# Routed experts: the weights become the stationary operand of gate and up, and the routing weights multiply the down products

## The chip, the cores and the metric

The kernel is one program on one core of a Trainium2 chip, written engine by engine with explicit semaphores: PE (TensorE) multiplies, ACT (ScalarE) and DVE (VectorE) empty PSUM, POOL (GpSimd) gathers, SP (SyncE) issues DMAs. The metric is the time of one execution on the device in microseconds (us), as the median of several runs.

## What is computed

Two transformer layers with gated residual branches. The change touches only the last branch, a mixture of experts (E = 32 experts, D = 256, inner width I = 128, T = 1024 tokens, 4 experts for each token, capacity C = 40 slots for each expert):

```python
G = jnp.einsum('ecd,edi->eci', Xp, W_gate)          # Xp: the C token rows of each expert
U = jnp.einsum('ecd,edi->eci', Xp, W_up)
Y = jnp.einsum('eci,eid->ecd', jax.nn.silu(G) * U, W_down)
Yf = Y.reshape(EC, d) * slots_w[:, None]            # routing weight of the slot
out = jnp.zeros((T, d), x.dtype).at[slots_token].add(Yf)
shared = jax.nn.silu(x @ shared_gate.T) * (x @ shared_up.T) @ shared_down.T
return (out + shared).reshape(b, s, d)
```

## The kernel before

The first layers and the latent attention fill the span up to about 363 us. Then `stage_moe` runs: the last projection, the norm, the router, the shared expert, the lists of slots, and from about 405 us the loop over the routed experts, which the change rewrites.

The loop takes the experts in 16 pairs (`PAIRED`). In a tile of 128 partitions, partitions 0 to 63 belong to the first expert of the pair and 64 to 127 to the second (`DC` = 64, of which 40 are slots). All matmuls of the loop are float32. For pair q:

- POOL gathers the 128 token rows with their routing weights from DRAM into `XR` (L1517).
- `turn_rows` (PE, L1620): two transposes, and ACT copies them to `XG` (`rows_turned`, L1735). `XG` has the input dimension on the partitions and 64 columns for each expert.
- `gate_up` (PE, L1634): for each of the two halves of the input dimension and each expert a matmul with the 64 columns of `XG` stationary and 256 columns of gate and up weights (`EGU`) moving. The result has the 64 slots of an expert on its partitions; the two experts use the two halves of the array's columns.
- `gated` (ACT, L1743): SiLU of the gate part to `SE`.
- `hidden` (DVE, L1891): two instructions of 64 partitions, `HR` = `SE` times routing weight (a column of `XR`) times the up part.
- `turn_hidden` (PE, L1647): one transpose of `HR`, copied by ACT to `HX` (`hidden_turned`, L1750).
- `down` (PE, L1658): two matmuls, the 64 columns of `HX` stationary, 256 columns of `ED` moving.
- `results` (ACT, L1755) writes the high float16 part to `YS`, `second` (DVE, L1900) the rest.
- `pack` (SP, L1456): two or three DMAs for each pair move `YS` to `YP`, in which slots lie without gaps. SP also issues the weights of the last experts (L1424, L1426).

The order of work is written out by hand, and each engine runs its own list in order. On PE:

```python
for q in range(PAIRED):
    if q + 2 < PAIRED:
        turn_rows(q + 2)
    if q + 1 < PAIRED:
        gate_up(q + 1)
    turn_hidden(q)
    if q == 1:
        pe.wait_ge(tok_ok, 1)
    if q >= 1:
        down(q - 1)
down(PAIRED - 1)
```

Before that loop PE runs `turn_rows(0)`, `turn_rows(1)`, `gate_up(0)` and a small transpose of the slot list (L1667), which waits for a DMA. After it comes `scatter` (L1684): 160 float16 matmuls with one-hot matrices add the packed rows to the tokens. The first 128 wait for the packing DMAs of pairs 0 to 12 (`d_pack[0]`), the last 32 for those of pairs 13 to 15. DVE then adds to `X` and SP stores.

Of the kernel before, what the change touches and what calls it, by code (L numbers as in the profile page):

```python
# [14 lines left out]
ALU = mybir.AluOpType  # L15
ACT = mybir.ActivationFunctionType
AX = mybir.AxisListType

P = 128
B, S, D = 4, 256, 256  # L20
T = B * S
NT = T // P
KT = D // P
# [3 lines left out]
DC = 64  # L27
# [13 lines left out]
E, EI = 32, 128  # L41
# [4 lines left out]
EPT = P // CAP  # L46
# [1252 lines left out]
def stage_moe(nc, g, i, out):  # L1299
# [11 lines left out]
    with ExitStack() as ctx:  # L1311
        sb = lambda name, shape, dt=F32: ctx.enter_context(nc.sbuf_tensor(name, shape, dt))
        sem = lambda name: ctx.enter_context(nc.semaphore(name))
        OWN, RING = 7, 9
# [34 lines left out]
        PAIRED = E // 2  # L1349
# [15 lines left out]
        EGU += [in_place(g.XT[:, :, :]), in_place(HS[:, :, :])]  # L1365
        ED += [g.XN[:, EPT * u:EPT * u + EPT, :] for u in range(RING - OWN)]
        SE = [sb(f"SE{u}", [P, EI]) for u in range(2)]
        HR = [sb(f"HR{u}", [P, EI]) for u in range(2)]
        HX = [sb(f"HX{u}", [P, P]) for u in range(2)]
        YS = [sb(f"YS{q}", [P, 2, D], F16) for q in range(PAIRED)]  # L1370
        rows_dram = nc.dram_tensor("token_rows", [T + 1, ROW], F32).ap()
# [6 lines left out]
        def pieces(e):  # L1378

            at, end, some = e * CAP, e * CAP + CAP, []  # L1380
            while at < end:
# [18 lines left out]
                  "sh_ps", "sh_ok"])  # L1400
        FLIGHT = 4
        d_g = [sem(f"d_g{q}") for q in range(FLIGHT)]
        (xt_ps2, xg_ok, gu_ps, se_ok, h_ok, ht_ps, hp_ok, st_ok, y_ps, yh_ok, yl_ok, acc_ps, fin_ok) = map(
            sem, ["xt_ps2", "xg_ok", "gu_ps", "se_ok", "h_ok", "ht_ps", "hp_ok", "st_ok", "y_ps2", "yh_ok", "yl_ok",
                  "acc_ps", "fin_ok"])
        d_pack = [sem("d_pack_early"), sem("d_pack_late")]

# [6 lines left out]
        with nc.Block() as block:  # L1414
# [107 lines left out]
            def _(pe):  # L1522
# [101 lines left out]
                def gate_up(q):  # L1624

                    pe.wait_ge(xg_ok, q + 1)
                    if q >= 2:
                        pe.wait_ge(h_ok, q - 1)
                    for e in (2 * q, 2 * q + 1):
                        pe.wait_ge(d_e[set_of(e // EPT)], landed(e // EPT))  # L1630
                    for k in range(KT):
                        for h in range(2):
                            e = 2 * q + h
                            mm = pe.matmul(g.ps[DC * h:DC * h + DC, GU + q % 2, 0:2 * EI],  # L1634
                                           XG[q % 2][:, k, DC * h:DC * h + DC],
                                           EGU[e // EPT % RING][:, e % EPT, k, :, :].rearrange("p w n -> p (w n)"),
                                           start=(k == 0), stop=(k == KT - 1))
                    mm.then_inc(gu_ps, 1)

                def turn_hidden(q):  # L1640

                    pe.wait_ge(h_ok, q + 1)
                    if q >= 2:
                        pe.wait_ge(hp_ok, q - 1)
                    else:
                        pe.wait_ge(sh_ok, q + 1)
                    pe.transpose(g.ps[:, HTB + q % 2, 0:P], HR[q % 2][:, :], g.ident[:, :]).then_inc(ht_ps, 1)  # L1647

                def down(q):

                    pe.wait_ge(hp_ok, q + 1)
                    if q >= 2:
                        pe.wait_ge(yl_ok, q - 1)
                    else:
                        pe.wait_ge(sh_ok, q + 3)
                    for h in range(2):
                        e = 2 * q + h
                        mm = pe.matmul(g.ps[DC * h:DC * h + DC, Y + q % 2, 0:D], HX[q % 2][:, DC * h:DC * h + DC],  # L1658
                                       ED[e // EPT % RING][:, e % EPT, :], start=True, stop=True)
                    mm.then_inc(y_ps, 1)  # L1660
# [8 lines left out]
                for q in range(PAIRED):  # L1669
                    if q + 2 < PAIRED:  # L1670
                        turn_rows(q + 2)
                    if q + 1 < PAIRED:
                        gate_up(q + 1)
                    turn_hidden(q)
                    if q == 1:
                        pe.wait_ge(tok_ok, 1)
                    if q >= 1:
                        down(q - 1)
                down(PAIRED - 1)

                acc = lambda t: half_bank(ACC, t)
                def scatter(t, n):
# [17 lines left out]
            @block.scalar  # L1700
            def _(act):
                def turned_norm(q):

                    act.wait_ge(xt_ps, q + 1)
                    act.activation(g.XT[:, :, S * q:S * q + S],
                                   g.ps[:, 4 + q % 2, :].rearrange("p (k s) -> p k s", k=KT),
                                   ACT.Copy).then_inc(xt, 1)

                def shared_gate(n):
                    act.wait_ge(gu_sh, 2 * n + 1)  # L1710
                    if n >= 2:
                        act.wait_ge(hs_ok, n - 1)
                    act.activation(SL[n % 2][:, :], g.ps[:, 2 * (n % 2), :], ACT.Silu).then_inc(sl_ok, 1)
                    act.wait_ge(gu_sh, 2 * n + 2)
                    act.activation(UPS[n % 2][:, :], g.ps[:, 2 * (n % 2) + 1, :], ACT.Copy).then_inc(sl_ok, 1)

                for q in range(B - 1):
                    norm_root(act, g, n3, q)
                turned_norm(0)
                turned_norm(1)  # L1720
                norm_root(act, g, n3, B - 1)
                turned_norm(2)
                act.activation(primed[:, :], g.gate[0:1, 0:1], ACT.Sigmoid)
                turned_norm(B - 1)
                act.wait_ge(rl_ps, 1)
                act.activation(SG[:, :, :], g.ps[:, 6, 0:NT * E], ACT.Sigmoid).then_inc(sg_ok, 1)
                for n in range(4):
                    shared_gate(n)

                def rows_turned(q):  # L1730

                    act.wait_ge(xt_ps2, q + 1)
                    if q >= 2:
                        act.wait_ge(gu_ps, q - 1)
                    act.activation(XG[q % 2][:, :, :], g.ps[:, XTB + q % 2, 0:D].rearrange("p (k s) -> p k s", k=KT),  # L1735
                                   ACT.Copy).then_inc(xg_ok, 1)

                def gated(q):

                    act.wait_ge(gu_ps, q + 1)  # L1740
                    if q >= 2:
                        act.wait_ge(h_ok, q - 1)
                    act.activation(SE[q % 2][:, :], g.ps[:, GU + q % 2, 0:EI], ACT.Silu).then_inc(se_ok, 1)  # L1743

                def hidden_turned(q):

                    act.wait_ge(ht_ps, q + 1)
                    if q >= 2:
                        act.wait_ge(y_ps, q - 1)
                    act.activation(HX[q % 2][:, :], g.ps[:, HTB + q % 2, 0:P], ACT.Copy).then_inc(hp_ok, 1)  # L1750

                def results(q):

                    act.wait_ge(y_ps, q + 1)
                    act.activation(YS[q][:, 0, :], g.ps[:, Y + q % 2, 0:D], ACT.Copy).then_inc(yh_ok, 1)  # L1755

                rows_turned(0)
                rows_turned(1)
                gated(0)
                for q in range(PAIRED):  # L1760
                    if q + 2 < PAIRED:
                        rows_turned(q + 2)
                    if q + 1 < PAIRED:
                        gated(q + 1)
                    hidden_turned(q)
                    if q >= 1:
                        results(q - 1)
                results(PAIRED - 1)

            @block.vector  # L1770
            def _(dve):
# [111 lines left out]
                def hidden(q):  # L1883

                    dve.wait_ge(d_g[q % FLIGHT], 16 * (q // FLIGHT + 1))
                    dve.wait_ge(se_ok, q + 1)
                    if q >= 2:
                        dve.wait_ge(ht_ps, q - 1)
                    for h in range(2):
                        rows = slice(DC * h, DC * h + DC)  # L1890
                        ins = dve.scalar_tensor_tensor(out=HR[q % 2][rows, :], in0=SE[q % 2][rows, :],  # L1891
                                                       scalar=XR[q % HOLD][rows, D + 2 * q + h:D + 2 * q + h + 1],
                                                       in1=g.ps[rows, GU + q % 2, EI:2 * EI], op0=ALU.mult,
                                                       op1=ALU.mult)
                    ins.then_inc(h_ok, 1)

                def second(q):

                    dve.wait_ge(yh_ok, q + 1)
                    dve.tensor_tensor(YS[q][:, 1, :], g.ps[:, Y + q % 2, 0:D], YS[q][:, 0, :],  # L1900
                                      ALU.subtract).then_inc(yl_ok, 1)

                hidden(0)
                dve.wait_ge(slot_ps, 2)
# [3 lines left out]
                for q in range(PAIRED):  # L1908
                    if q + 1 < PAIRED:
                        hidden(q + 1)  # L1910
                    if q >= 1:
                        second(q - 1)
                    if 3 <= q < 3 + TILES_S:
                        placed(q - 3)
                second(PAIRED - 1)
                for b in range(B):
                    dve.wait_ge(acc_ps, 2 * b + 2)
                    for t in (2 * b, 2 * b + 1):
# [110 lines left out]
```

## Time and profile before

| | us |
|---|---|
| median of 3 runs (464.79 to 466.34) | 465.26 |
| the profiled execution, time | 466.26 |
| its span, first to last instruction | 464.5 |
| PE busy | 432.4 (93%) |
| DVE busy | 301.3 (65%) |
| ACT busy | 252.4 (54%) |
| POOL busy | 193.9 (42%) |
| routed loop, from the slot transposition to the scatter | 408.57 to 443.34 |

The span leaves out 1.8 us of the execution's own time. Busy time is the time in which an engine has an instruction in flight, so PE at 93% isn't PE at its peak. Weight loads are shown as an engine of their own (PEld). A float32 matmul appears as two instructions, each with its own weight load; a float32 transpose as one.

### The profile page before, as it was taken

The page shows a single profiled execution, that of the slowest core. Times are in us where ns is not written, and L with a number is a line of the kernel's source. Part 1 is how long each engine was busy: PE and PEld are TensorE (multiplying, and loading weights), DVE is VectorE, ACT ScalarE, POOL GpSimd, SP SyncE. Part 2 cuts the span into 40 slices and gives each one's busy share as a digit, 9 for nine tenths or more (in the row PEclk, how much of TensorE's full clock was granted, in tenths as well). Part 3 has the DMA queues.
Part 4 walks back from the last instruction along what each step waited for, and adds up shares of the span by engine and source line. Part 5 has one row for each costly group of instructions (what it writes and reads, how often), then busy time and mean ns, then how long its engine had stood idle before and what let it go on. Part 6 is the DMA issues. An engine that isn't in the chain of part 4 may idle for free. (4 is left out here: it accounts for less than half of the span.)

```text
span 464.5 us, 8843 instructions
## 1 busy us (share of the span) xinstructions
PE 432.4 (93%) x2723; PEld 276.3 (59%) x2723; DVE 301.3 (65%) x880; ACT 252.4 (54%) x629; POOL 193.9 (42%) x195
## 2 busy tenths in 40 slices
PE   5895999989988999999999999999999998889996
PEld 2584787777744555556555555555568773644476
DVE  3979799965247757667676667757744558446613
ACT  3593336364344776767677766776666252145500
POOL 3441314040434556565456655556644425444000
PEclk9996899999999999999999999999999999999999
DMA  7743000000204343443324334212200599789202
GB/s 249 218 97 102 1 1 2 1 1 2 68 0 97 78 107 76 94 122 68 98 71 102 90 76 104 57 44 52 64 23 2 148 308 305 210 203 244 65 30 92
DMA packets 61448, 43.81 MB, mean 94 GB/s; under 512 B 22955, under 2 KB 54502, under 8 KB 61414
## 3 DMA queue, kind: packets, MB, share of 16 engines
q1 hardware_dynamic: 60646, 41.04, 33.2%
q0 software_dynamic: 768, 2.36, 2.6%
q8 instruction: 17, 0.28, 0.3%
q14 instruction: 17, 0.14, 0.1%
HBM read 27.25 MB, written 2.23 MB: 63 GB/s over the span
## 5 line engine op out<-in xcount | busy, mean ns | idle before, releaser
L1206 POOL TENSOR_TENSOR W1T<-W1T,inv 128x512 f32<-128x512 f32 x64 | 66.5, 1039 | 77.4 <-DVE inv L1261 77.4
L1150 ACT ACTIVATE W1T<-ps,low 128x256 f32<-128x256 f32 x128 | 59.5, 470 | 30.8 <-DVE low L1255 30.8
L276 POOL TENSOR_TENSOR rot<-rot 128x512 f32<-128x512 f32 x48 | 61.0, 1270 | 28.7 <-DMA rot<-rot 28.7
L1255 DVE TENSOR_REDUCE low<-ps 128x2 f32<-128x512 f32 x64 | 44.1, 688 | 39.2 <-PE ps L1065 38.6
L1158 ACT ACTIVATE W2T<-ps 128x512 f32<-128x512 f32 x64 | 38.2, 597 | 7.2 <-PE ps L1073 5.2
L1073 PE MATMUL ps<-ident,W1T 128*128 128x128 f32 x256 | 41.1, 283 | 0.9 <-POOL W1T L1206 0.8
L1073 PEld LDWEIGHTS ps<-ident,W1T 128*128 128x128 f32 x256 | 27.8, 141 | 23.7 <-issue 20.3
L256 DVE TENSOR_TENSOR rot<-ps,sinq 128x512 f32<-128x512 f32 x48 | 33.1, 690 | 13.4 <-PE ps L243 11.2
L243 PE MATMUL ps<-XH,CH 128*128 128x512 f16 x96 | 36.4, 379 | 0.9 <-DVE XL L862 0.9
L243 PE MATMUL ps<-XL,CH 128*128 128x512 f16 x96 | 36.4, 379 | 0.0
L243 PE MATMUL ps<-XH,CL 128*128 128x512 f16 x96 | 36.4, 379 | 0.0
L1082 PE MATMUL ps<-W2T,KV 128*64 128x256 f32 x256 | 34.7, 392 | 0.0
L675 PE MATMUL ps<-XT,W1T 128*128 128x256 f32 x128 | 33.3, 411 | 0.0
L257 DVE TENSOR_TENSOR rot<-ps,cosq 128x512 f32<-128x512 f32 x48 | 32.6, 680 | 0.0
L1065 PE MATMUL ps<-KH,Q 128*128 128x256 f16 x128 | 31.4, 273 | 0.0
L1065 PE MATMUL ps<-KL,Q 128*128 128x256 f16 x128 | 31.4, 273 | 0.0
L675 PEld LDWEIGHTS ps<-XT,W1T 128*128 128x128 f32 x128 | 25.4, 205 | 4.3
L906 DVE MAX8 m<-work 128x8 f32<-128x256 f32 x72 | 26.8, 413 | 0.0
L911 DVE MATCH_REPLACE8 work<-m,work 128x256 f32<-128x256 f32 x64 | 25.7, 408 | 0.0
L1150 ACT ACTIVATION_READ_ACCUMULATOR W1T<-ps,low 128x1 f32 x128 | 25.3, 198 | 0.0
L134 PE MATMUL ps<-NH,wide 128*128 128x256 f16 x128 | 23.1, 273 | 1.0 <-PEq L1984 0.8
L302 DVE TENSOR_TENSOR Q<-ps,Q 64x512 f16<-64x512 f32 x32 | 22.0, 688 | 1.2 <-ACT Q L294 0.5
(247 smaller groups left out, 863.5 us busy)
## 6 DMA issues: line engine op xcount, KB each, us to landing
rot<-rot SPq DMA_DIRECT2D x64, 128.0 KB, 2.3
rot<-rot SPq DMA_DIRECT2D x64, 64.0 KB, 2.0
EGU<-in_L_ffn_W_gate_dram SPq DMA_DIRECT2D x8, 384.0 KB, 5.9
EGU<-in_L_ffn_W_up_dram SPq DMA_DIRECT2D x8, 384.0 KB, 5.8
ED<-in_L_ffn_W_down_dram SPq DMA_DIRECT2D x8, 384.0 KB, 6.1
rot<-in_L_ffn_W_dram SPq DMA_DIRECT2D x2, 1024.0 KB, 8.4
WQ<-in_L_xattn_Wq_dram SPq DMA_DIRECT2D x8, 256.0 KB, 2.9
WO<-in_L_xattn_Wo_dram SPq DMA_DIRECT2D x8, 256.0 KB, 3.1
```

The costliest lines, as they stand in the source:

```text
L243: mm = pe.matmul(g.ps[:, bank, :], cx[:, c, x * P:(x + 1) * P], xx[:, c, 512 * n:512 * n + 512], start=(c == 0 and m == 0), stop=(c == KT ...
L256: dve.tensor_tensor(batches(g.TS[x][:, :]), src, over(g.sinq), ALU.mult).then_inc(g.sin_ok, 1)
L257: dve.tensor_tensor(batches(g.TC[x][:, :]), src, over(g.cosq), ALU.mult).then_inc(g.rope_ok, 1)
L276: pool.tensor_tensor(g.RO[:, n, x, :], g.RO[:, n, x, :], g.TC[x][:, :], ALU.add).then_inc(g.sum_ok, 1)
L675: mm = pe.matmul(g.ps[:, HB + u % 2, S * o:S * o + S], W1T[:, k, (2 * n + o) * P:(2 * n + o + 1) * P], XT[b % 2][:, k, :], start=(k == 0), ...
L1065: mm = pe.matmul(g.ps[:, SC + t % 2, S * h:S * h + S], g.Q[h][u][:, t * P:(t + 1) * P], kx[:, S * (t // 2):S * (t // 2) + S], start=(m == ...
L1073: mm = pe.transpose(g.ps[:, PTB, j * P:(j + 1) * P], PB[t % 2][:, j // 2, (j % 2) * P:(j % 2 + 1) * P], g.ident[:, :])
L1082: mm = pe.matmul(g.ps[DC * h:DC * h + DC, CXB, 0:S], g.KV[:, 2 * b + j, 0, :], PTS[b % 2][:, 2 * h + j, :], start=(j == 0), stop=(j == 1))
L1150: e = act.activation(PB[t % 2][:, h, :], g.ps[:, SC + t % 2, h * S:(h + 1) * S], ACT.Exp, bias=low[:, t % 2, h:h + 1], scale=-1.0, accum_o ...
L1158: act.activation(PTS[t // 2 % 2][:, :, (t % 2) * P:(t % 2 + 1) * P], g.ps[:, PTB, :].rearrange("p (j n) -> p j n", j=4), ACT.Copy).then_in ...
L1206: pool.tensor_tensor(PB[t % 2][:, :, :], PB[t % 2][:, :, :], inv[:, t % 2, :].unsqueeze(2).broadcast_to([P, 2, S]), ALU.mult).then_inc(nor ...
L1255: dve.tensor_reduce(low[:, t % 2, :], g.ps[:, SC + t % 2, :].rearrange("p (h s) -> p h s", h=2), AX.X, ALU.min).then_inc(low_ok, 1)
```

## The change

`gate_up` swaps its operands: for each expert, each of gate and up, and each half of the input dimension, a 128x128 block of `EGU` is stationary and the 64 columns of `XG` move. The result has the inner dimension on the partitions, the gate in PSUM columns 0 to 127 and the up part in 128 to 255, with 64 columns for each expert. It is what `down` needs, so `turn_hidden`, `hidden_turned`, `HR` and their semaphores go. The routing weight now belongs to a column and not to a partition at that place; so DVE copies the two columns of weights into `WS`, multiplies `SE` by the up part straight into `HX`, and `results` and `second` multiply by `WS` when they empty the down products. `down(q)`, `results(q)` and `second(q)` move from step q + 1 of the loop to step q.

```diff
--- before.py
+++ after.py
@@ -1365,7 +1365,7 @@
         EGU += [in_place(g.XT[:, :, :]), in_place(HS[:, :, :])]
         ED += [g.XN[:, EPT * u:EPT * u + EPT, :] for u in range(RING - OWN)]
         SE = [sb(f"SE{u}", [P, EI]) for u in range(2)]
-        HR = [sb(f"HR{u}", [P, EI]) for u in range(2)]
+        WS = sb("WS", [P, PAIRED])
         HX = [sb(f"HX{u}", [P, P]) for u in range(2)]
         YS = [sb(f"YS{q}", [P, 2, D], F16) for q in range(PAIRED)]
         rows_dram = nc.dram_tensor("token_rows", [T + 1, ROW], F32).ap()
@@ -1400,8 +1400,8 @@
                   "sh_ps", "sh_ok"])
         FLIGHT = 4
         d_g = [sem(f"d_g{q}") for q in range(FLIGHT)]
-        (xt_ps2, xg_ok, gu_ps, se_ok, h_ok, ht_ps, hp_ok, st_ok, y_ps, yh_ok, yl_ok, acc_ps, fin_ok) = map(
-            sem, ["xt_ps2", "xg_ok", "gu_ps", "se_ok", "h_ok", "ht_ps", "hp_ok", "st_ok", "y_ps2", "yh_ok", "yl_ok",
+        (xt_ps2, xg_ok, gu_ps, se_ok, h_ok, ws_ok, st_ok, y_ps, yh_ok, yl_ok, acc_ps, fin_ok) = map(
+            sem, ["xt_ps2", "xg_ok", "gu_ps", "se_ok", "h_ok", "ws_ok", "st_ok", "y_ps2", "yh_ok", "yl_ok",
                   "acc_ps", "fin_ok"])
         d_pack = [sem("d_pack_early"), sem("d_pack_late")]
 
@@ -1628,27 +1628,18 @@
                         pe.wait_ge(h_ok, q - 1)
                     for e in (2 * q, 2 * q + 1):
                         pe.wait_ge(d_e[set_of(e // EPT)], landed(e // EPT))
-                    for k in range(KT):
-                        for h in range(2):
-                            e = 2 * q + h
-                            mm = pe.matmul(g.ps[DC * h:DC * h + DC, GU + q % 2, 0:2 * EI],
-                                           XG[q % 2][:, k, DC * h:DC * h + DC],
-                                           EGU[e // EPT % RING][:, e % EPT, k, :, :].rearrange("p w n -> p (w n)"),
-                                           start=(k == 0), stop=(k == KT - 1))
+                    for h in range(2):
+                        e = 2 * q + h
+                        for w in range(2):
+                            at = EI * w + DC * h
+                            for k in range(KT):
+                                mm = pe.matmul(g.ps[:, GU + q % 2, at:at + DC], EGU[e // EPT % RING][:, e % EPT, k, w, :],
+                                               XG[q % 2][:, k, DC * h:DC * h + DC], start=(k == 0), stop=(k == KT - 1))
                     mm.then_inc(gu_ps, 1)
 
-                def turn_hidden(q):
+                def down(q):
 
                     pe.wait_ge(h_ok, q + 1)
-                    if q >= 2:
-                        pe.wait_ge(hp_ok, q - 1)
-                    else:
-                        pe.wait_ge(sh_ok, q + 1)
-                    pe.transpose(g.ps[:, HTB + q % 2, 0:P], HR[q % 2][:, :], g.ident[:, :]).then_inc(ht_ps, 1)
-
-                def down(q):
-
-                    pe.wait_ge(hp_ok, q + 1)
                     if q >= 2:
                         pe.wait_ge(yl_ok, q - 1)
                     else:
@@ -1671,12 +1662,9 @@
                         turn_rows(q + 2)
                     if q + 1 < PAIRED:
                         gate_up(q + 1)
-                    turn_hidden(q)
-                    if q == 1:
+                    if q == 0:
                         pe.wait_ge(tok_ok, 1)
-                    if q >= 1:
-                        down(q - 1)
-                down(PAIRED - 1)
+                    down(q)
 
                 acc = lambda t: half_bank(ACC, t)
                 def scatter(t, n):
@@ -1742,17 +1730,11 @@
                         act.wait_ge(h_ok, q - 1)
                     act.activation(SE[q % 2][:, :], g.ps[:, GU + q % 2, 0:EI], ACT.Silu).then_inc(se_ok, 1)
 
-                def hidden_turned(q):
-
-                    act.wait_ge(ht_ps, q + 1)
-                    if q >= 2:
-                        act.wait_ge(y_ps, q - 1)
-                    act.activation(HX[q % 2][:, :], g.ps[:, HTB + q % 2, 0:P], ACT.Copy).then_inc(hp_ok, 1)
-
                 def results(q):
 
                     act.wait_ge(y_ps, q + 1)
-                    act.activation(YS[q][:, 0, :], g.ps[:, Y + q % 2, 0:D], ACT.Copy).then_inc(yh_ok, 1)
+                    act.activation(YS[q][:, 0, :], g.ps[:, Y + q % 2, 0:D], ACT.Copy,
+                                   scale=WS[:, q:q + 1]).then_inc(yh_ok, 1)
 
                 rows_turned(0)
                 rows_turned(1)
@@ -1762,10 +1744,7 @@
                         rows_turned(q + 2)
                     if q + 1 < PAIRED:
                         gated(q + 1)
-                    hidden_turned(q)
-                    if q >= 1:
-                        results(q - 1)
-                results(PAIRED - 1)
+                    results(q)
 
             @block.vector
             def _(dve):
@@ -1884,21 +1863,21 @@
 
                     dve.wait_ge(d_g[q % FLIGHT], 16 * (q // FLIGHT + 1))
                     dve.wait_ge(se_ok, q + 1)
-                    if q >= 2:
-                        dve.wait_ge(ht_ps, q - 1)
                     for h in range(2):
                         rows = slice(DC * h, DC * h + DC)
-                        ins = dve.scalar_tensor_tensor(out=HR[q % 2][rows, :], in0=SE[q % 2][rows, :],
-                                                       scalar=XR[q % HOLD][rows, D + 2 * q + h:D + 2 * q + h + 1],
-                                                       in1=g.ps[rows, GU + q % 2, EI:2 * EI], op0=ALU.mult,
-                                                       op1=ALU.mult)
-                    ins.then_inc(h_ok, 1)
+                        dve.tensor_copy(WS[rows, q:q + 1], XR[q % HOLD][rows, D + 2 * q + h:D + 2 * q + h + 1]
+                                        ).then_inc(ws_ok, 1)
+                    if q >= 2:
+                        dve.wait_ge(y_ps, q - 1)
+                    dve.wait_ge(ws_ok, 2 * q + 2)
+                    dve.tensor_tensor(HX[q % 2][:, :], SE[q % 2][:, :], g.ps[:, GU + q % 2, EI:2 * EI],
+                                      ALU.mult).then_inc(h_ok, 1)
 
                 def second(q):
 
                     dve.wait_ge(yh_ok, q + 1)
-                    dve.tensor_tensor(YS[q][:, 1, :], g.ps[:, Y + q % 2, 0:D], YS[q][:, 0, :],
-                                      ALU.subtract).then_inc(yl_ok, 1)
+                    dve.scalar_tensor_tensor(out=YS[q][:, 1, :], in0=g.ps[:, Y + q % 2, 0:D], scalar=WS[:, q:q + 1],
+                                             in1=YS[q][:, 0, :], op0=ALU.mult, op1=ALU.subtract).then_inc(yl_ok, 1)
 
                 hidden(0)
                 dve.wait_ge(slot_ps, 2)
@@ -1908,11 +1887,9 @@
                 for q in range(PAIRED):
                     if q + 1 < PAIRED:
                         hidden(q + 1)
-                    if q >= 1:
-                        second(q - 1)
+                    second(q)
                     if 3 <= q < 3 + TILES_S:
                         placed(q - 3)
-                second(PAIRED - 1)
                 for b in range(B):
                     dve.wait_ge(acc_ps, 2 * b + 2)
                     for t in (2 * b, 2 * b + 1):
```

On PE, in the middle of the loop, one pair is four rows before (names are output<-moving,stationary; the size is that of the output, so 64x256 is one expert's half of the array):

```order
L1620 MATMUL ps<-ident,XR 128x128 x2
L1634 MATMUL ps<-EGU,XG 64x256 x4
L1647 MATMUL ps<-ident,HR 128x128
L1658 MATMUL ps<-ED,HX 64x256 x2
L1620 MATMUL ps<-ident,XR 128x128 x2
L1634 MATMUL ps<-EGU,XG 64x256 x4
L1647 MATMUL ps<-ident,HR 128x128
L1658 MATMUL ps<-ED,HX 64x256 x2
```

and three rows after:

```order
L1620 MATMUL ps<-ident,XR 128x128 x2
L1636 MATMUL ps<-XG,EGU 128x64 x8
L1649 MATMUL ps<-ED,HX 64x256 x2
L1620 MATMUL ps<-ident,XR 128x128 x2
L1636 MATMUL ps<-XG,EGU 128x64 x8
L1649 MATMUL ps<-ED,HX 64x256 x2
```

Four matmuls of 256 moving columns became eight of 64, the transpose of `HR` went, and `down` follows the `gate_up` of the next pair directly.

On DVE, in the middle of the loop, before (`wide` is the one-hot matrix, `placed`):

```order
L1891 SCALAR_TENSOR_TENSOR HR<-SE,XR,ps 64x128 x2
L1900 TENSOR_TENSOR YS<-ps,YS 128x256
L1880 TENSOR_SCALAR wide<-tokf,slot_tok 128x1024
L1891 SCALAR_TENSOR_TENSOR HR<-SE,XR,ps 64x128 x2
L1900 TENSOR_TENSOR YS<-ps,YS 128x256
```

and after:

```order
L1868 COPY WS<-XR 64x1 x2
L1873 TENSOR_TENSOR HX<-SE,ps 128x128
L1879 SCALAR_TENSOR_TENSOR YS<-ps,WS,YS 128x256
L1859 TENSOR_SCALAR wide<-tokf,slot_tok 128x1024
L1868 COPY WS<-XR 64x1 x2
L1873 TENSOR_TENSOR HX<-SE,ps 128x128
L1879 SCALAR_TENSOR_TENSOR YS<-ps,WS,YS 128x256
```

Two multiplications of 64 partitions became two copies of one column and one multiplication of 128 partitions; `second` has a per-partition multiplier.

## Rows read from the trace of the kernel before

**Rows 1.** The page's first part: busy us (share of the span) and instructions.

```profile
PE 432.4 (93%) x2723; PEld 276.3 (59%) x2723; DVE 301.3 (65%) x880; ACT 252.4 (54%) x629; POOL 193.9 (42%) x195
```

**Rows 2.** Chain that ended last, from 436 us: start us, us, what.

```profile
436.23 0.58 PE ps L1658 x4
436.81 0.37 PE ps L1620 x2
437.18 1.01 PE ps L1634 x8
438.19 0.26 PE ps L1647
438.45 0.61 PE ps L1658 x4
...
439.95 0.71 SPq L1456
...
441.46 1.74 DMA wide<-YS
...
443.34 15.02 PE ps L1684 x136
```

**Rows 3.** Stretches, PE: us, busy (instructions), granted clock, DMA share, GB/s.

```profile
40.00:44.00 4.00, 2.55 (x11) 0.50 0.28 58
...
374.90:379.30 4.40, 4.12 (x38) 1.00 1.16 306
...
408.57:439.90 31.33, 31.33 (x216) 1.00 0.69 170
```

**Rows 4.** Timeline, three of the eight instructions of one `gate_up`.

```profile
434.89 0.43 PE L1634 MATMUL ps<-HS,XG 128*64 128x256 f32 x1
...
434.89 0.43 PE L1634 MATMUL ps<-EGU,XG 128*64 128x256 f32 x1
...
435.58 0.38 PE L1634 MATMUL ps<-HS,XG 128*64 128x256 f32 x1
```

**Rows 5.** Timeline, matmuls with 128x128 float32 weights: start, us, line, out<-in, stationary, moving.

```profile
377.54 1.95 PE L1560 MATMUL ps<-rwT,XT 128*128 128x32 f32 x16
379.33 7.11 PE L1544 MATMUL ps<-XT,shT 128*128 128x512 f32 x16
...
32.16 0.39 PE L590 MATMUL ps<-wide,ident 128*128 128x128 f32 x2
32.38 0.39 PE L589 MATMUL ps<-ident,wide 128*128 128x128 f32 x2
```

**Rows 6.** Timeline, the start of the loop on PE.

```profile
405.84 1.08 PE L1634 MATMUL ps<-EGU,XG 128*64 128x256 f32 x8
...
408.41 0.22 PE L1667 MATMUL ps<-ident,slot_raw 10*128 10x10 f32 x1 [1.49 <-DMA slot_raw<-slot_rows]
...
408.57 0.44 PE L1620 MATMUL ps<-ident,XR 128*128 128x128 f32 x2
```

**Rows 7.** Timeline, the end of the loop.

```profile
439.94 0.28 ACT L1743 ACTIVATE SE<-ps 128x128 f32<-128x128 f32 x1 [0.48 <-PE ps L1634]
...
441.07 0.33 PE L1647 MATMUL ps<-ident,HR 128*128 128x128 f32 x1 [0.34 <-DVE HR L1891]
...
441.33 1.09 PE L1658 MATMUL ps<-ED,HX 128*64 128x256 f32 x8
```

**Rows 8.** Groups by form: count, busy us, mean ns of one, idle before.

```profile
L1261 DVE RECIPROCAL inv<-tot 128x2 f32<-128x2 f32 x64 | 10.1, 158 | 19.5 <-ACT W1T L1150 19.5
L1249 DVE TENSOR_TENSOR wide<-ps,wide 128x256 f32 x24 | 10.0, 416 | 1.9 <-ACT wide L1164 1.9
...
L1150 ACT ACTIVATE W1T<-ps,low 128x256 f32<-128x256 f32 x128 | 59.5, 470 | 30.8 <-DVE low L1255 30.8
```

**Rows 9.** Timeline, SP's queue: issues of the packing DMAs.

```profile
413.27 1.64 SPq L1456 DMA_DIRECT2D wide<-YS  x2
...
421.21 25.93 SPq L1456 DMA_DIRECT2D wide<-YS  x35
```

## The prediction

> **What bounds the kernel now.** I read the page's busy times first. PE has an instruction in flight for 93% of the span [rows 1], which says that PE matters and not yet what it waits for. The change touches only the routed loop, so I read that end of the chain of waits [rows 2]. In the loop the chain stays on PE, piece after piece without a wait: `down` 0.58 us, `turn_rows` 0.37, `gate_up` 1.01, `turn_hidden` 0.26, together 2.22 us for a pair. Then it leaves PE: from the `down` of pair 12 (438.45) to its packing DMAs (439.95 to 441.46) and the landing, 1.74 us later; the scatter starts at 443.34. So the loop costs what PE's list costs up to pair 12, plus a tail of DMAs behind which PE ends the last pairs. The table of stretches [rows 3] has PE busy for all of 408.57 to 439.90, at a granted clock of 1.00, which is 2.4 GHz.
>
> **What one `gate_up` costs after the change.** Before, it is eight instructions (float32: two for each matmul) of 256 moving columns, but they run two and two: both experts' instructions start at 434.89, since each uses its own half of the array, and the last pair of them starts at 435.58 [rows 4]. The block takes 1.01 us [rows 2]. After, it is 8 matmuls, so 16 instructions, each with 128x128 weights and 64 moving columns, on the whole array and one after another. Neither this shape nor its pitch stands in the trace; both neighbours do. Router logits with 128x128 float32 weights and 32 moving columns: 16 instructions from 377.54 to the next line at 379.33 [rows 5], 0.112 us each. The same weights with 128 moving columns: two instructions from 32.16 to 32.38 [rows 5], 0.11 us each. Four times the columns cost nothing, so at these sizes something other than the columns sets the pitch, and every instruction has a weight load of its own. At 64 columns I take 0.112: 16 x 0.112 = 1.79 us. Columns alone would give the same as before: 0.11 us for 128 columns makes 0.055 for 64, and 16 of those are 0.88 us.
>
> The Trainium skill (TensorE: Matmul & The Clock Gate, section "Back-to-back issue gap") gives about 60 cycles, some 25 ns, as the gap for 1 to 64 columns. By it alone the block would be 0.4 us, an estimate from the page, and the change would be faster. The same page's section "LDWEIGHTS" has a load take its columns divided by 1.2, so 107 ns for 128, whatever the matmul does; with it the estimate is 1.71 us. The trace's 0.112 agrees with the second.
>
> **The other terms of a pair on PE.**
> - `turn_hidden` goes: 0.26 us less [rows 2].
> - Changes between whole-array and half-array work. Two transposes at 0.11 us would be 0.22, but `turn_rows` takes 0.37 before a half-array `gate_up`; one is 0.11, but `turn_hidden` takes 0.26 before `down` [rows 2, 5]. So about 0.15 us is lost on going into halves. After the change `gate_up` uses the whole array: `turn_rows` costs 0.22, and 0.15 is lost once, ahead of `down`.
> - `down` itself is unchanged and so is what follows it: 0.58 us.
>
> Sum: 0.22 + 1.79 + 0.15 + 0.58 = 2.74 us for a pair, against 2.22: +0.52.
>
> The Trainium skill (TensorEngine Tiling (Array Packing), "Key Properties") says that a change of tiling mode drains the engine; the 0.15 us agrees. Its section "When to Use Tiling" advises, where the moving side has 64 columns or fewer, to swap the operands and use two column tiles. That is the kernel before; by the page the change goes the wrong way.
>
> **From pair to span.** `gate_up(0)` grows by 0.78 us but starts at 405.84, and PE's next work waits for the slot list until 408.41 [rows 6]: 405.84 + 1.79 = 407.63, so it is hidden, with 0.78 us to spare. The loop proper starts at 408.57. After the change steps 0 to 13 each hold all three blocks: 14 x 2.74 = 38.36, to 446.93. Step 14 has `gate_up(15)`, to 448.72, then 0.15 and `down(14)`, to 449.45. `down(15)` needs pair 15's hidden rows. Before, SiLU started at 439.94 and the PE instruction that needed `HR` at 441.07 [rows 7], 1.13 us with 0.28 of SiLU, 0.71 of DVE and hand-offs of 0.14. The new DVE part is two copies of one column (the nearest small row is 0.158 [rows 8]; between nothing and 0.32 together), and one multiplication of 128x128 from PSUM: between 0.158 (two columns) and 0.416 (256 columns) [rows 8], 0.29 taken, as it lies in the middle. With a wait of DVE for itself, about 0.06, it is 0.28 + 0.3 + 0.29 + 0.2 = 1.07, so `down(15)` starts at 448.72 + 0.06 + 1.07 = 449.85, 0.4 late, and with 0.58 PE is free for the scatter at 450.43.
>
> Are the packing DMAs ready by then? `down(12)` would start at 408.57 + 12 x 2.74 + 2.16 = 443.61. Before, 1.5 us lay between its start and the first issue and 3.3 more up to landing [rows 2]: 448.4 to 448.6. So the DMAs are 1.9 us early and the 0.9 us in which PE now waits for them is gone. The scatter starts at 450.43 instead of 443.34: **+7.1 us**. Behind it nothing changes: the scatter itself (15.02 us for its chain part [rows 2]), additions and stores; the last packs have some 10 us.
>
> **What I cost at nothing.** In the loop ACT loses a copy of 128x128 (as the SiLU, 0.28 us) for each pair; `results` gains a per-partition multiplier. A copy of 128x256 with such an operand takes 0.470 [rows 8], so ACT has about 0.4 + 0.28 + 0.47 in 2.74 us. DVE has two copies, 0.29, about 0.48 for `second` and the one-hot, under 1.8 us. Both are covered by PE. The hidden rows of pair q have, up to `down(q)`, the 0.73 of `down(q-1)`, 0.22 and 1.79: 2.74 us for a chain of 1.1. If a wait were left anyway, each 0.1 us of it would cost 1.4 us over 14 steps. SP's queue was close to full: 35 issues back to back in 25.93 us, 0.74 each [rows 9]. With more time for each pair it has more room.
>
> **Rivals.**
> 1. *Load and columns add up.* If the 64 columns (0.055 us) came on top of the load, 0.165 us an instruction, `gate_up` would be 2.64 us, and 15 blocks cost 12.8 us more than forecast: 485. Against it: with 128 columns they don't add [rows 5]. A small part of it, 0.12 instead of 0.112, would be +1.9. Chance 6% for anything above 475.5.
> 2. *Faster: columns set the pitch.* If loads hid wholly behind 64 columns, `gate_up` would be 0.88 us and a pair 1.83. Then PE is no longer the bound: SP is, with 33 packing issues up to pair 12 at 0.74 plus six of weights, some 28 us from the first pack. That pack comes from about 411.2 instead of 413.27 [rows 9], so the scatter starts some 2.1 us earlier: 463.2. It wins if the pitch is below about 0.075, where the pair costs under 2.2 us. For it speak the page's gap of 25 ns and a PE that is 93% busy; against it the logits with only 32 columns at 0.112. 3%.
> 3. *The clock falls.* Fewer columns stream in each us. At 1.2 GHz a pair would take about 5.4 us: 510. The one such stretch, 0.50 at 40.00 to 44.00 [rows 3], came after PE had idled for 4 us; the logits with 32 columns kept 1.00. 2%.
> 4. *The DMAs stay the bound, or nothing changes.* If PE's end of the loop were shorter than I make it, the packing of pair 12 would still come 443.61 - 438.45 = 5.2 us later, so the scatter can't start before 448.5: 470.4. No change at all needs a pair of 2.22 us, so a pitch of 0.08. 2% for that.
>
> **Numbers.** The profiled execution took 466.26 us, 1.0 above the median 465.26; +7.1 on its own time is 473.4, on the median **472.4**. My case, 87%: between 470.8 (pitch 0.107, no copies) and 474.5 (pitch 0.117, a little wait). The range, for 8 in 10, is 470.3 to 475.5. Measurements of this kernel tell about 0.3%, 1.4 us. Slower by more than that: my case and rivals 1 and 3, 95%; within it 2%; faster 3%.
>
> **What would show it.** In the profile after: 16 `gate_up` instructions a pair at a pitch of 0.11 us and a block of 1.8; `turn_rows` at 0.22; a period of 2.74; weight loads busy for most of the loop; no wait of PE for the packing DMA before the scatter, and a short one for `HX` before the last `down`. The prediction is wrong if the pitch isn't 0.11, or if PE waits for DVE or ACT inside the loop.

## The result, and the profile after

The changed kernel took 472.0 us against 465.2: slower by a factor of 1.0137 (95% interval 1.0109 to 1.0165). The forecast was 472.4, in a range of 470.3 to 475.5. Of its four executions one took 506.55 us, at a mean granted TensorE clock of 0.909 instead of 0.989, and the ratio leaves it out.

The profiled execution took 472.03 us, 5.8 more than that of before. The page's first part, which answers to [rows 1]:

```profile
PE 440.8 (94%) x2835; PEld 296.0 (63%) x2835; DVE 300.4 (64%) x896; ACT 249.1 (53%) x613; POOL 194.3 (41%) x195
```

PE has 112 matmul instructions more and 8 us more of busy time (440.8 against 432.4). The chain that ended last, at the end of the loop, answers to [rows 2]:

```profile
440.01 0.37 PE ps L1620 x2
440.38 1.73 PE ps L1636 x16
442.12 0.58 PE ps L1649 x4
...
445.38 1.94 PE ps L1636 x16
...
447.35 0.29 ACT SE L1731
...
447.73 0.15 DVE WS L1868
...
447.90 0.16 DVE WS L1868
...
448.16 0.30 DVE HX L1873
...
448.50 0.65 PE ps L1649 x4
449.15 14.97 PE ps L1672 x136
```

A pair is 0.37 + 1.73 + 0.58 = 2.68 us where it was 2.22. The chain stays on PE until the last `gate_up`, goes once through SiLU, copies and multiplication, and enters the scatter straight from the last `down`: the packing DMA of before is gone from it. The chain counts a block from the end of the one before; the timeline has the starts:

```profile
426.53 0.44 PE L1620 MATMUL ps<-ident,XR 128*128 128x128 f32 x2
...
426.80 1.90 PE L1636 MATMUL ps<-XG,EGU 128*128 128x64 f32 x16
...
428.63 0.65 PE L1649 MATMUL ps<-ED,HX 128*64 128x256 f32 x4
...
429.21 0.44 PE L1620 MATMUL ps<-ident,XR 128*128 128x128 f32 x2
```

From start to start it is 0.27, 1.83 and 0.58. The `gate_up` block covers 1.90 us, of which its last instruction takes 0.27 (mean below), so the last one starts 1.63 after the first: 15 steps of 0.109 us. From there to `down` are 0.20, so 0.09 more than a step.

The groups by form, in the loop (count, busy us, mean ns of one; the weights lie in three tiles, of which `EGU` is one). PEld, the weight loads, is busy for 32.5 of the 39.4 us from 408.57 to 448.00.

```profile
L1636 PE MATMUL ps<-XG,EGU 128*128 128x64 f32 x185 | 22.3, 272 | 0.0
L1636 PEld LDWEIGHTS ps<-XG,EGU 128*128 128x128 f32 x183 | 21.5, 192 | 0.4 <-issue 0.4
...
L1736 ACT ACTIVATE YS<-ps,WS 128x256 f16<-128x256 f32 x15 | 7.1, 475 | 4.7 <-PE ps L1649 4.7
...
L1868 DVE COPY WS<-XR 64x1 f32<-64x1 f32 x30 | 4.4, 148 | 18.8 <-ACT SE L1731 12.2 <-DMA XR<-token_rows,idx 6.2
L1873 DVE TENSOR_TENSOR HX<-SE,ps 128x128 f32<-128x128 f32 x15 | 4.3, 289 | 1.5
```

The start of the loop, which answers to [rows 6]:

```profile
405.41 2.00 PE L1636 MATMUL ps<-XG,EGU 128*128 128x64 f32 x16
407.59 0.23 PE L1658 MATMUL ps<-ident,slot_raw 10*128 10x10 f32 x1 [0.17 <-DMA slot_raw<-slot_rows]
407.74 0.44 PE L1620 MATMUL ps<-ident,XR 128*128 128x128 f32 x2
```

Here the slot list's DMA landed 0.8 us earlier than in the profiled execution of before, in a part of the program that the change doesn't touch. From the loop's first transposes to the scatter it is 407.74 to 449.09, 41.35 us, against 34.77 before: **+6.6 us**. Less the 0.8 of the earlier start this is the 5.8 between the two profiled executions; the medians, with 6.8, are nearer to the 6.6.

### The profile page after: what moved, and what is told of

The parts are those of the page before. It is cut to its first block and busy times, and to the rows that moved or that the text cites. A ratio compares the mean times of both kernels' runs of the same rounds, so it can differ in the third digit from the quotient of the medians.

```text
span 470.2 us, 9051 instructions
## 1 busy us (share of the span) xinstructions
PE 440.8 (94%) x2835; PEld 296.0 (63%) x2835; DVE 300.4 (64%) x896; ACT 249.1 (53%) x613; POOL 194.3 (41%) x195
## 5 line engine op out<-in xcount | busy, mean ns | idle before, releaser
L1636 PE MATMUL ps<-XG,EGU 128*128 128x64 f32 x208 | 25.0, 273 | 0.1
L1636 PEld LDWEIGHTS ps<-XG,EGU 128*128 128x128 f32 x208 | 24.3, 192 | 0.7 <-issue 0.4
```

Of the source, the lines that this page charges most:

```text
L1636: mm = pe.matmul(g.ps[:, GU + q % 2, at:at + DC], EGU[e // EPT % RING][:, e % EPT, k, w, :], XG[q % 2][:, k, DC * h:DC * h + DC], start=(k ...
```

## The experiments

Each was timed beside the kernel before on the same chip, though not all on the same one, so a ratio says more than a time. All ratios are to the kernel before.

**The changed kernel again.** No edit.

> The changed kernel unaltered, beside the kernel before. Theory: the loop over the routed experts costs 6.6 us more (a pair on TensorE 2.68 us instead of 2.22), so the ratio should be 1.014 (472.0 against 465.2). Rival: the 5.8 us between the two profiled executions is the true cost, and the ratio is 1.012. A second point: the granted clock. If fewer streaming columns let the clock fall, some executions show a mean clock well under 0.98 and a time near 505 us in this kernel and none in the kernel before.

472.23 us against 465.09, ratio 1.0143 (1.0121 to 1.0165), or 6.7 us (5.6 to 7.7). That agrees with the loop's 6.6. The 5.8 of the two profiled executions lies just inside the interval, so this run alone doesn't rule it out; the later run of the same kernel, with 1.0126 as its lower end (5.9 us), just does. One execution took 507.62 us, at a mean clock of 0.912.

**Twice the columns.**

```diff
-                            at = EI * w + DC * h
+                            at = P * (2 * h + w)
...
-                                mm = pe.matmul(g.ps[:, GU + q % 2, at:at + DC], ...,
-                                               XG[q % 2][:, k, DC * h:DC * h + DC], ...)
+                                mm = pe.matmul(g.ps[:, GU + q % 2, at:at + P], ...,
+                                               XG[q % 2][:, k, :], ...)
```

SiLU and the multiplication then pick out the half that is needed, in two instructions each where there was one.

> The changed kernel with 128 moving columns instead of 64 in gate and up (both experts' tokens stream through each expert's weights; the half that isn't needed is never read; SiLU and the multiplication take two instructions each). Theory, the load sets the pitch up to 128 columns: 0.11 us an instruction, the time stays within 1.5 us of the changed kernel, 472 to 473.5 us. Rival, load and columns add up: 0.053 us more an instruction, 16 instructions and 15 pairs, 485 us.

471.92 us, level with the changed kernel (ratios 1.0152 and 1.0143, and the intervals overlap). Its chain:

```profile
436.35 0.37 PE ps L1620 x2
436.71 1.79 PE ps L1636 x16
438.50 0.58 PE ps L1649 x4
```

Twice the columns cost 1.79 - 1.73 = 0.06 us a block, 4 ns an instruction. The 64 columns that the change streams are wholly hidden behind something that each instruction pays.

**Fewer columns.**

```diff
-                                mm = pe.matmul(g.ps[:, GU + q % 2, at:at + DC], ...,
-                                               XG[q % 2][:, k, DC * h:DC * h + DC], ...)
+                                mm = pe.matmul(g.ps[:, GU + q % 2, at:at + CAP], ...,
+                                               XG[q % 2][:, k, DC * h:DC * h + CAP], ...)
```

> The changed kernel with 40 moving columns in gate and up instead of 64 (the 40 that are slots; columns 40 to 63 of the hidden tile keep what was there, and their rows are never packed). Theory, the load of the 128x128 weights sets the pitch: 0.109 us an instruction as with 64, a pair 2.68 us, 472 us. Rival, load and columns add up in part: 24 columns less at 2 cycles are 0.02 us an instruction, 0.32 us a pair, 467 us.

506.45 us, in all six executions between 504.3 and 507.9: ratio 1.088 (1.0857 to 1.0905). Neither the theory (472) nor its rival (467) had this. The stretches of PE say why (us, busy (instructions), granted clock, DMA share, GB/s):

```profile
380.00:404.00 24.00, 22.14 (x84) 1.00 1.01 283
404.00:410.00 6.00, 4.64 (x30) 0.86 0.66 160
410.00:420.00 10.00, 10.00 (x47) 0.50 0.48 127
...
440.00:470.00 30.00, 30.00 (x136) 0.50 0.15 37
```

The clock falls to 0.50, 1.2 GHz, at about 408.3, as the loop begins, and is back at 1.00 only at about 487, 3.5 us into the scatter. From 404 up to the fall PE waited three times, 0.64, 0.17 and 0.62 us; from there to 482.20, in the last `down`, it was busy for 73.8 of 73.9 us. Those waits alone don't explain the fall: in the same place the kernel before waited 1.33 us for a gather and 1.49 us for the slot list [rows 6] and kept 1.00. Before the fall the timeline has a short block at full clock, and then the same block in almost twice the time:

```profile
405.48 1.98 PE L1636 MATMUL ps<-XG,EGU 128*128 128x40 f32 x16 [0.17 <-ACT XG L1723]
408.08 0.23 PE L1658 MATMUL ps<-ident,slot_raw 10*128 10x10 f32 x1 [0.62 <-DMA slot_raw<-slot_rows]
...
408.68 3.47 PE L1636 MATMUL ps<-XG,EGU 128*128 128x40 f32 x16
412.08 1.12 PE L1649 MATMUL ps<-ED,HX 128*64 128x256 f32 x4
```

At full clock 40 columns take 1.98 us where 64 took 2.00, so fewer columns save nothing either. A pair takes 4.94 us, 2.26 more than with 64 columns; over 15 pairs that is the 34 us between the two kernels.

**The changed kernel once more, for the clock.**

> The changed kernel unaltered once more, for the clock: of 9 executions so far 2 were near 507 us with a mean granted clock of 0.91 (none of 44 of the kernel before, all 6 with 40 columns, none of 5 with 128). [...] Rival: the two were disturbances from outside and none comes.

472.11 us, ratio 1.0143 (1.0126 to 1.016), and one of four executions at 505.95 with a mean clock of 0.912. In all, such an execution came 3 times in 13 of the changed kernel, 6 times in 6 of `cols40`, never in 5 of `cols128` and never in 55 of the kernel before. So it belongs to these kernels and isn't a disturbance that any kernel would meet. Two things aren't shown. No trace of a slow execution with 64 columns was kept: that it is the same fall rests on its mean clock and time, which are those of `cols40`. And with 3 in 13, none in 5 is no proof that 128 columns are safe.

The trace of `cols128` even has a short fall, in a part that no edit touches. It comes right behind the router logits, matmuls with 128x128 weights and 32 moving columns; PE had waited 0.28 us in the 4.4 us before the fall (stretches of PE, the logits first):

```profile
376.12:377.90 1.78, 1.78 (x18) 1.00 1.18 304
378.00:381.40 3.40, 3.40 (x5) 0.51 1.18 314
381.50:404.00 22.50, 21.40 (x85) 1.00 0.96 268
```

In the profiled executions of the kernel before and of the changed kernel the clock is 1.00 in the same place.

**Half of the change alone.** Gate, up and the transpose as before; the routing weights multiply the down products (in `second` too, which is left out here).

```diff
-                    act.activation(YS[q][:, 0, :], g.ps[:, Y + q % 2, 0:D], ACT.Copy).then_inc(yh_ok, 1)
+                    act.activation(YS[q][:, 0, :], g.ps[:, Y + q % 2, 0:D], ACT.Copy,
+                                   scale=WS[:, q:q + 1]).then_inc(yh_ok, 1)
...
-                        ins = dve.scalar_tensor_tensor(out=HR[q % 2][rows, :], ...)
+                        dve.tensor_copy(WS[rows, q:q + 1], XR[q % HOLD][rows, ...])
...
+                    dve.tensor_tensor(HR[q % 2][:, :], SE[q % 2][:, :], g.ps[:, GU + q % 2, EI:2 * EI], ALU.mult)
```

> The kernel before with the second half of the change alone: the routing weights multiply the down products, gate and up and the transpose of the hidden rows stay. Theory: all of the loss is TensorE's operand swap, and this half is covered; 465.2 us, within 1 us. Rival: the per-partition multiplier on ScalarE (0.47 instead of 0.38 us) and the copies on VectorE cost something in the loop or on the way to the packing, 466.5 us or more.

465.83 us, ratio 1.0012 (0.9997 to 1.0027): no difference that can be told. The chain from the `down` of pair 12 to its packing:

```profile
437.61 0.61 PE ps L1659 x4
438.24 0.48 ACT YS L1756
438.75 0.50 DVE YS L1902
439.26 0.71 SPq L1457
```

That way is 1.65 us long and was 1.50 [rows 2]; it lies on the path in this kernel, which could give 0.15 us. So the loss lies in the operand swap; the interval leaves at most 1.3 us for this half.

**The wait for the packing DMAs.** The kernel before with

```diff
-        FULL = TILES_S - 2
+        FULL = TILES_S - 4
```

> The kernel before, with the scatter's first part over 6 of the 10 slot tiles instead of 8, so that it waits for the packing DMAs of pairs 0 to 9 and not 0 to 12. Theory: the kernel before loses 0.9 us there, because the packing DMAs of pair 12 are later than TensorE's end of the loop, and the changed kernel doesn't pay this. The scatter starts 0.9 us earlier and the rest of the packs is landed before its first part of 10.5 us ends: 464.2 against 465.1. Rival: the wait only moves to the second part, no change.

464.11 us, ratio 0.9973 (0.9956 to 0.9989), or 1.3 us less (0.5 to 2.0). The scatter follows `down` at once:

```profile
441.20 1.02 PE ps L1658 x8
442.22 17.59 PE ps L1684 x160
```

So the kernel before loses about 1 us in that wait (0.9 in its trace), and the changed kernel doesn't pay it.

**What the passages cost.** The kernel before, with the transpose of the hidden rows behind that of the gathered rows (ACT's list follows):

```diff
                         turn_rows(q + 2)
+                    if q >= 1:
+                        turn_hidden(q - 1)
                     if q + 1 < PAIRED:
                         gate_up(q + 1)
-                    turn_hidden(q)
```

> The kernel before, with the transpose of the hidden rows of pair q - 1 put right behind the transposes of the gathered rows, so that TensorE has one stretch of whole-array and one of half-array work for each pair instead of two and two. No work is added or removed. Theory: each passage between the two costs 0.1 to 0.15 us, so a pair falls from 2.22 us to 1.9 or 2.0 on TensorE; but the packing DMAs of SyncE's queue (33 issues and 6 of weights up to pair 12, 28 us) then hold the scatter, so that only 0.3 to 1 us comes out: 464.5. Rival: the gaps belong to the waits between blocks and not to the passages; a pair stays at 2.22 and the time at 465.1.

467.18 us, ratio 1.0023 (0.9998 to 1.0048): no gain. PE waits 3.3 us for the packing, and the scatter then runs at a lower clock (waits: us, times, longest; and stretches of PE):

```profile
PE ps L1686 <- DMA wide<-YS: 3.3, 1, 3.3
```

```profile
436.00:441.00 5.00, 2.43 (x16) 1.00 0.15 48
442.00:447.00 5.00, 4.46 (x22) 0.50 0.15 46
```

The expected 464.5 was missed. TensorE is done earlier and waits longer, and while it waits the clock falls to 0.50; the scatter's first 136 matmuls then take 17.88 us instead of 15.02. The executions bear it out: the two with a mean clock of 0.989 took 464.75 and 463.88 us, as expected, the ten at 0.977 to 0.985 took 465.2 to 469.4. Without the wait, in the next kernel, the clock doesn't fall. With `FULL` at 6 tiles as well:

> Both edits together. Theory: with the scatter's first part waiting for pairs 0 to 9 alone, the 0.25 to 0.3 us saved on each of 14 pairs come out whole, plus the 0.9 us of the wait: 460 to 461 us. Rival: SyncE's queue binds the second part as well, 463 us or more.

462.5 us, ratio 0.994 (0.9916 to 0.9964), between the 460 to 461 expected and the rival's 463. The chain:

```profile
428.10 1.01 PE ps L1634 x8
429.11 0.43 PE ps L1658 x4
429.54 0.37 PE ps L1620 x2
430.02 1.01 PE ps L1634 x8
```

A pair from start to start is 430.02 - 428.10 = 1.92 us instead of 2.22, with the same matmuls. It has two passages less between whole-array and half-array work, one in and one out, and they are worth 0.30, 0.15 each. The gain is smaller than 14 times that, since gathers now hold PE, 1.8 us in two waits.

**The swap in halves.** The changed kernel with each weight block in two halves of the array:

```diff
+                                for j in range(2):
+                                    half = slice(DC * j, DC * j + DC)
-                                mm = pe.matmul(g.ps[:, GU + q % 2, at:at + DC], EGU[...][:, e % EPT, k, w, :], ...)
+                                    mm = pe.matmul(g.ps[half, GU + q % 2, at:at + DC],
+                                                   EGU[...][:, e % EPT, k, w, half], ...)
```

> The changed kernel with each 128x128 weight block loaded as two blocks of 64 columns, one into each half of the array, which then stream the same 64 columns side by side (32 instructions for a pair instead of 16). Theory: the load sets the pitch, a load of 64 columns takes half as long (in the down products two such loads start 0.06 us after the two before them) and the two halves load at the same time; gate and up take about 1.0 us instead of 1.73, and since down then works in halves too, a pair takes 1.85 to 1.95 us. The packing DMAs bind before that: 464 us. Rival: it isn't the load but the number of instructions that sets the pitch, so 32 instructions take as long as before or longer: 472 us or more.

467.48 us, ratio 1.0052 (1.0037 to 1.0068), where 464 was expected. Its chain leaves PE before the scatter for the packing DMAs, as that of `grouped` does, and here too the clock is 0.50 from 442 to 445: the first 136 matmuls of the scatter take 16.68 us instead of 15.02. PE also waits 4.1 us for gathers inside the loop. With `FULL` at 6 tiles:

> The same with the scatter's first part over 6 slot tiles. Theory: TensorE's end of the loop now counts whole, 14 pairs at 1.85 to 1.95 us: 461 to 462 us, the best of all, level with grouped_full6 (462.5) or a little under it. Rival: the gathers or SyncE's queue keep a pair above 2 us: 463 us or more. If the clock falls as with 40 columns, 490 us.

462.65 us, ratio 0.9942 (0.9924 to 0.9959), level with `grouped_full6` and about 9 us under the changed kernel. The chain of this last kernel:

```profile
429.80 0.37 PE ps L1620 x2
430.17 1.08 PE ps L1638 x32
431.25 0.43 PE ps L1653 x4
431.69 0.37 PE ps L1620 x2
```

`gate_up` takes 1.08 us with 32 instructions, where the changed kernel took 1.73 with 16. So it isn't the count of instructions that costs. The weights loaded are the same, and the same 64 columns stream through each half; what differs is that two loads of 64 columns run side by side, one for each half. The weight loads themselves are shorter, 0.138 us instead of 0.192:

```profile
L1638 PEld LDWEIGHTS ps<-XG,EGU 128*64 128x64 f32 x384 | 12.3, 138 | 2.0 <-issue 1.9
```

With `cols128` and the full-clock block of `cols40` this leaves the width of the stationary block, and so its load, as what sets the pitch: 40, 64 and 128 moving columns cost nearly the same, and half the stationary columns cost less. A step of two instructions is 0.068 us (1.08 / 16), though, and not half of 0.109; what else is in it stays open.

## Why the prediction was right, and where its numbers were off

**The pitch of `gate_up`.** Forecast 0.112 us from the neighbours with 32 and 128 columns; measured 0.109. It was the step on which all hung, and taking it from rows on both sides, with 32 and 128 columns, settled it. Rival 1 (load and columns add up) fell with `cols128`: 64 columns more cost 4 ns and not 53. Rival 2 (columns set the pitch) fell with the profile after, and `halves` points to the load as the bound.

**The passages.** Forecast was 0.15 us for each way into halves. `grouped_full6` gives 0.15 as a mean over a way in and a way out, so the ways out cost as well; the prediction didn't name them, but counted from start to start one lay inside the 0.58 of `down`, which it carried over whole. In the changed kernel the way ahead of `down` costs only 0.09, and `turn_rows`, where no passage was reckoned with, takes 0.27 instead of 0.22; why isn't shown. Block by block: 0.27 + 1.83 + 0.58 = 2.68 against 0.22 + 1.94 + 0.58 = 2.74. The two misses on the passages nearly cancel, and the smaller pitch is 0.05 of the 0.06. The 14 full steps took 37.57 us (407.74 to 445.31) and not 38.36, 0.8 less.

**The first `gate_up` is hidden.** Right, but with less room: the transposition of the slot list ran at 407.59, and PE had waited 0.17 us for it, not 0.78. With a block 0.2 us longer it would have been on the path in this execution.

**The end of the loop.** From the SiLU's start to the last `down` I had 1.07 us; it is 448.50 - 447.35 = 1.15. Copies 0.148 each and the multiplication 0.289 are as taken. The hand-offs between them are a little longer. PE waited 0.6 us for it, not 0.4. From the last full step to the scatter it was 3.78 us against 3.50 forecast, 0.3 more.

**The packing DMAs.** As forecast, PE has no wait before the scatter. `full6` puts the wait of before at about 1 us.

**The sum.** +7.1 forecast, +6.6 in the loop and +6.8 between medians. So the forecast of 472.4 was 0.3 too high by the sum and 0.1 by the median of before, which came out at 465.19. The mechanism was right; that the total came out this close is in part luck, since the pairs were 0.8 us too long and the end 0.3 too short.

**The clock (rival 3).** It had 2%, and 510 us. Its size was near (506 to 508 us in 3 of 13 executions), its chance too small: I had only asked what lowered the clock in the trace of before, an idle PE [rows 3], and took a stage of 4 us with 32 columns at 1.00 as a sign that thin matmuls keep it. A loop ten times as long isn't that case, and in the trace of `cols128` the clock fell right behind that very stage. The forecast holds for the executions at full clock.

## What to carry to other kernels

When small matmuls swap operands, count weight loads and not columns: a float32 matmul with 128x128 weights costs two steps of 0.11 us here whether 32 or 128 columns follow. Before choosing the stationary side, look whether both halves of the array can load and stream side by side, and put blocks of the same kind next to each other. And after such a swap look at the granted clock of several executions, not of one.

## What the runs showed of the hardware that was not expected

TensorE's clock fell to 1.2 GHz at the start of a loop and stayed there for all of it, though from the fall on PE had an instruction in flight nearly all the time: in 6 of 6 executions with 40 moving columns, and by time and mean clock also in 3 of 13 with 64. At the lower level a pair with 40 columns took 4.94 us, where one with 64 at full clock took 2.68. The Trainium skill (TensorE: Matmul & The Clock Gate, section "HAM oscillation — how this bites in real kernels") speaks of idle gaps of PE as what brings the clock down. The falls in `grouped` and `halves` came during or right behind such a gap, as PE waited 3.3 and 1.1 us for the packing. The one in `cols40` had only waits of up to 0.64 us ahead of it, where the kernel before kept 1.00 through 1.49 us, and it outlasted 73.8 us of busy time, so here the runs decide. Why it falls stays open: between `cols40` and the changed kernel only the moving columns differ, yet one was hit every time and the other now and then.

A multiplier for each partition on ACT made a copy of 128x256 take 0.475 us instead of 0.383, as `scale_only` had reckoned with. The Trainium skill (ScalarE: Activation LUTs, section "What ACT_TABLE_LOAD costs") adds about 93 ns for such an operand, which agrees.
